# Window attention with an MLP: VectorE does the mean's subtraction ahead of the second low part of U, and the bias addition ahead of the next strip's second maximum

## What is computed

```python
qkv = (xw @ qkv_w + qkv_b)...            # q, k, v of each window
attn = softmax(einsum('bhnd,bhmd->bhnm', q, k) * dh ** -0.5 + bias)
out = einsum('bhnm,bhmd->bhnd', attn, v)... @ proj_w + proj_b
x = x + xr                               # xr: out, put back in image order
xn = layernorm(x, norm2_g, norm2_b)
x = x + gelu(xn @ fc1_w + fc1_b) @ fc2_w + fc2_b
```

## Time and profile before

| | before |
|---|---|
| median of three runs | 1924.84 us (1924.18 to 1928.86) |
| the profiled execution | 1922.45 us |
| its span in the profile | 1920.8 us |
| TensorE busy | 1741.0 us, 91% of the span |
| VectorE busy | 1593.1 us, 83% |
| ScalarE busy | 1536.0 us, 80% |
| GpSimd busy | 1245.8 us, 65% |

### The profile page before, as it was taken

How to read it: one execution, slowest core, us unless ns; L and a number is a source line. 1 busy time by engine, 2 the same in 40 slices (tenths; PEclk the granted TensorE clock), 3 DMA queues, 4 the chain that set the end, 5 groups by cost and what they waited for, 6 DMA issues and landing times. The chain is left out here.

```text
span 1920.8 us, 90622 instructions
## 1 busy us (share of the span) xinstructions
PE 1741.0 (91%) x38180; PEld 1035.6 (54%) x38180; DVE 1593.1 (83%) x2134; ACT 1536.0 (80%) x3090; POOL 1245.8 (65%) x1048
## 2 busy tenths in 40 slices
PE   5999999999999999999999999996999968998996
PEld 3656656665565666656566566651577743333332
DVE  6899889999999999899989999864777757888883
ACT  3788888888888888888888888884666649888881
POOL 5788888888888888888888888763355540221222
PEclk9999999999999999999999999995899985999998
DMA  4343554434444443444444343423488759999994
GB/s 115 90 114 97 151 132 111 111 98 111 102 117 105 106 115 96 117 100 118 102 111 112 101 115 99 98 57 70 112 215 216 214 145 177 240 253 257 263 256 143
DMA packets 233230, 262.25 MB, mean 137 GB/s; under 512 B 167078, under 2 KB 179910, under 8 KB 232710
## 3 DMA queue, kind: packets, MB, share of 16 engines
q1 hardware_dynamic: 217478, 217.47, 46.8%
q0 software_dynamic: 15360, 39.08, 6.7%
HBM read 160.79 MB, written 80.88 MB: 126 GB/s over the span
## 5 line engine op out<-in xcount | busy, mean ns | idle before, releaser
L425 POOL TENSOR_TENSOR shift<-const_b,qmax 113x588 bf16<-113x588 bf16 x256 | 413.9, 1617 | 219.6 <-DVE qmax L520 219.6
L512 DVE TENSOR_TENSOR Ul<-Uf 113x784 bf16<-113x784 f32 x192 | 260.2, 1381 | 0.0
L520 DVE TENSOR_REDUCE qmax<-ps_s 113x12 f32<-113x588 f32 x256 | 195.4, 763 | 50.6 <-PE ps_s L917 46.8
L1537 POOL DMA_DIRECT2D out_rolled<-r_OUT x128 | 63.8, 503 | 264.3 <-DVE r_OUT L1606 264.3
L1378 PE MATMUL conv_ps<-xin,band_now 64*64 64x448 bf16 x2688 | 202.8, 364 | 2.2 <-DVE x_low L1256 2.2
L731 ACT ACTIVATE P<-ps_t 113x588 f32<-113x588 f32 x256 | 170.0, 664 | 39.0 <-PE ps_t L969 36.6
L724 ACT COPY Uf<-ps_m 113x392 f32<-113x392 f32 x384 | 172.8, 485 | 29.7 <-PE ps_m L882 21.6
L741 ACT COPY V<-ps_t 49x192 f32<-49x192 f32 x512 | 168.8, 330 | 8.8 <-PE ps_t L969 2.4
L984 PEld LDWEIGHTS ps_o<-P,V 113*32 113x32 f32 x6144 | 108.0, 109 | 103.4 <-ACT P L731 52.4
L762 ACT ACTIVATE G<-ps_m 128x392 f32<-128x392 f32 x256 | 113.9, 502 | 46.5 <-PE ps_m L1023 46.2
L984 PE MATMUL ps_o<-P,V 113*32 113x49 f32 x6144 | 141.6, 210 | 8.7 <-DVE O L531 2.7
(11 more groups left out here) (233 smaller groups left out, 5324.2 us busy)
## 6 DMA issues: line engine op xcount, KB each, us to landing
xin<-rows_scratch SPq DMA_DIRECT2D x96, 236.0 KB, 3.7
XT<-x_tokens SPq DMA_DIRECT2D x64, 294.0 KB, 3.5
X<-x_windows SPq DMA_DIRECT2D x128, 147.0 KB, 3.3
RS<-rs_scratch SPq DMA_DIRECT2D x128, 147.0 KB, 3.1
XR<-x_windows SPq DMA_DIRECT2D x128, 147.0 KB, 3.1
x_scratch<-x SPq DMA_DIRECT2D x128, 147.0 KB, 3.4
y_scratch<-y POOLq DMA_DIRECT2D x96, 196.0 KB, 2.8
r_RS<-rs_scratch SPq DMA_DIRECT2D x128, 147.0 KB, 4.3
```

Source lines behind the costliest of these rows:

```text
L425: nc.gpsimd.tensor_tensor(shift[:, j % 2], e, m, ALU.mult).then_inc(S["md"], 1)
L512: nc.vector.tensor_tensor(Ul[:, r, h, :], Uf[:, r, h, :], U[0][:, r, h, :], ALU.subtract).then_inc(S["u_lo"], 1)
L520: nc.vector.tensor_reduce(qmax[:, j % 2, :].rearrange("p (b n) -> p b n", b=2), ps_s[0:R, :, 0:2 * HQ].rearrange("p b (n t) -> p b n t", t ...
```

## The change

In VectorE's step, `subtract_mean(prv)` and `u_low(nxt, 1)` change places, and `add_bias(prv)` goes ahead of `query_max(nxt, 1)`, directly behind `u_low(nxt, 2)`. No instruction is added, removed or altered, and no other engine's program is touched.

```diff
                 divide(s, 0)
                 u_low(nxt, 0)
+                subtract_mean(prv)
                 u_low(nxt, 1)
-                subtract_mean(prv)
                 query_max(nxt, 0)
                 divide(s, 1)
                 square(prv)
                 u_low(nxt, 2)
+                add_bias(prv)
                 query_max(nxt, 1)
-                add_bias(prv)
```

## The result

| | before | after |
|---|---|---|
| median | 1924.51 us (4 runs, 1919.32 to 1928.86) | 1955.4 us (4 runs, 1953.0 to 1958.35) |
| the profiled execution | 1922.45 us | 1953.0 us |
| its span | 1920.8 us | 1951.3 us |
| first to last second_residual | 1237.5 us | 1264.5 us |

The ratio is 1.0169 [1.0141, 1.0198]: slower, and by more than the rival on the other side had given (1942). 27.0 of the 30.5 us between the two spans lie in the attention phase. The other 3.5 are in phases whose instructions are the same; between the runs of before the time moves by 9.5.

What follows compares the result with a forecast made beforehand. TensorE was taken to stand twice in fc1 because of VectorE, whose second low part waits for GpSimd's memory use. Profiled 1922.45 - 35.6 - 1 = 1885.9, median 2.4 above: 1888 us; range 1880 to 1932.

Steps and rivals of the forecast that it cites:

- the rival on the other side: Centring on GpSimd takes the memory before the second low part; qmax 0.32 later per strip, 1942 us; chance 0.22.
- Step 1: Attention phase, subtract_mean ahead of the second low part: VectorE gets the memory, qmax starts earlier, 35.6 us gained.
- Step 2: Attention phase, add_bias ahead of the second maximum: fits a VectorE wait, costs 0, gains 0.02 per strip, 1 us.
- the side effect: Early add_bias makes GpSimd's chain 0.2 later, t_mean passes the shift, next divide earlier: 0 to 0.2 gained per strip.
- The mild form of the rival: GpSimd takes the memory first, but add_bias's effect brings low1 forward some 0.2: loss 0.1 per strip, 1930 us.
- The rival "no change": What is won ahead of fc1 is given back before the next strip: 1925 us; chance 0.10.
- 54 strips by 0.66: Size of the subtract_mean move's gain: 54 normal strips, each 0.66 us shorter, 35.6 us in all.

Runs made afterwards that it cites:

- mean_gap: Kernel before with subtract_mean ahead of the second low part, and GpSimd's centring moved behind the third shift, where GpSimd stood idle: 1905.89 us, ratio 0.9901.
- gap_only: Kernel before with only GpSimd's centring moved behind the third shift, VectorE's order unchanged: 1942.22 us, ratio 1.0088.
- mean_only: Kernel before with only subtract_mean moved ahead of the second low part, add_bias in its old place: 1941.97 us, ratio 1.0075.
- bias_only: Kernel before with only add_bias moved ahead of the second maximum: 1936.66 us, ratio 1.0065.
- pause11: Kernel before with subtract_mean ahead of the second low part and eleven tiny GpSimd memsets between low1 and centring: 1921.69 us.
- pause16: Kernel before with subtract_mean ahead of the second low part and sixteen tiny GpSimd memsets between low1 and centring: 1916.81 us, ratio 0.9986.
- halves: Kernel before with only the first half of subtract_mean moved ahead of the second low part: 1911.01 us, ratio 0.993.
- wrap_behind: Kernel before with subtract_mean ahead of the second low part, and GpSimd's two wrap_columns copies moved between low1 and centring: 1963.91 us, ratio 1.0228.
- divide_22: Kernel before with VectorE's order subtract_mean, second divide, second low part, and 22 tiny GpSimd memsets between low1 and centring: 1928.66 us.

## Why the prediction was wrong

**Step 1, the contest for the memory, failed.** The sum put VectorE first with 0.68, on the reading that "what counts seems to be whether VectorE's preceding instruction has started, as if the claim were made then". That rested on one case behind a t_var and one against a divide that had not started, neither with a subtract_mean ahead. The 62 contests of the shift with square, behind a divide, bear the reading out but have no subtract_mean ahead either. And the earlier trace rows lies at the edge: at 38 us a centring was issued 0.16 behind t_var's start and 0.60 ahead of normalise0 in both mean_gap and gap_only; it waited in the one (2.73) and ran in the other (1.31). Here that instruction had started 0.31 ahead of centring (0.47 ahead of the low part), the time of issue was as forecast (0.16 against 0.17), and GpSimd won in every normal strip. Behind subtract_mean the claim comes after the low part's own start, which is the point at which the prediction said its rival decides. Why it comes earlier behind a divide stays open. The rival's price was right: 0.32 a strip, 1942; mean_only measured 1941.97.

The rule of the Trainium skill (SBUF — State Buffer, Who interferes with whom), that the one that issues first gets the shared port pair, gave the right winner here, and by it the sum was 1942. The runs agree with it in all 298 cases behind subtract_mean with GpSimd first. They disagree in both directions. GpSimd also won when it was issued up to 0.12 us after the low part. Behind a divide it lost though it was issued up to 0.15 (centring) and 0.26 (low1) ahead, and behind a t_var though 0.60 ahead.

**Step 2, the side effect, had the wrong sign.** The prediction saw that add_bias, granted at once, makes GpSimd's chain 0.2 later, and that was right (the shift comes 2.95 after the strip's start; 2.73 in the earlier trace rows). It then said that t_mean "would be ahead of the shift" and cheaper. t_mean is issued at 718.32, 0.03 ahead of the shift's 718.35, and yet takes 1.22: it ends behind the shift. So 0.03 ahead isn't enough for VectorE. That fits the offset of the contests behind subtract_mean, but is not shown to be the same thing: when t_mean was issued, GpSimd was still at the small copy of 718.17 (0.22), right behind which the shift came. What depends on t_mean moves by 0.22: normalise0, the maximum of the fourth quarter, GpSimd's x1_low and low1, and centring and the second low part behind low1. bias_only shows that alone, +0.22 a strip. The term was a gain of 0.02 and measured a loss of 0.22. The mild form of the rival (low1 earlier, 0.1 a strip) had the same sign error.

**The range** ended at 1932, with 0.21 for slower; even its left-out 1942 would have missed the two losses together.

**What held, and how far.** Once the low part has the memory, it takes 0.96 and qmax follows, as mean_gap shows. The three full strips at the end of the phase, in which there is no centring any more, show the same in the changed kernel itself. VectorE:

```profile
1261.62 1.04 DVE L587 TENSOR_TENSOR x<-ps_m,x 112x392 f32<-112x392 f32 x2 [1.79 <-PE ps_m L1042]
...
1273.93 0.96 DVE L512 TENSOR_TENSOR Ul<-Uf 113x784 bf16<-113x784 f32 x1
...
1280.71 1.04 DVE L587 TENSOR_TENSOR x<-ps_m,x 112x392 f32<-112x392 f32 x2 [1.79 <-PE ps_m L1042]
```

They are 19.09 apart, close to the 19.05 of the forecast, but that is no measure of the gain, since these strips have no token statistics either. The same three strips of the kernel before are 19.54, 19.52 and 19.06 apart; VectorE's rows of the first:

```profile
1216.09 1.04 DVE L587 TENSOR_TENSOR x<-ps_m,x 112x392 f32<-112x392 f32 x2 [0.19 <-issue]
...
1225.72 3.15 DVE L512 TENSOR_TENSOR Ul<-Uf 113x784 bf16<-113x784 f32 x2
...
1235.63 1.04 DVE L587 TENSOR_TENSOR x<-ps_m,x 112x392 f32<-112x392 f32 x2 [0.20 <-issue]
```

So the reordering wins 0.45 and 0.43 in two of them and nothing in the third, where the low parts weren't held up before either. In the changed kernel's normal strips subtract_mean comes 11.52 after the start with an idle of 0.52 released by TensorE (11.3 and 0.5 were forecast), fc1's first part no longer waits for xc, and add_bias takes 0.61 at once. The rival "no change" is out: from qmax to the next second_residual are 5.89 us (729.78 to 735.67), as before, so that what is lost ahead of fc1 is not given back. Neither is a gain: in a normal strip of mean_gap it is 5.90. The prediction's last part named the outcome: "centring lasts 1.31, the second low part about 2"; its strips of 19.8 to 20.05 lacked only the second loss.

**The size was too kind too:** 54 strips by 0.66. Where the low part does take 0.96, normal strips are 19.2 apart (mean_gap 19.22, pause11 and pause16 19.21), 0.50 to 0.52 less than before. The 0.66 rested on one strip, the one at 1058.67, with its late start of 0.28 counted as gain in full, and no run reached it. The long strips, for which the sum had no term, then took a third to a half of what was left: mean_gap came out 19 us ahead of before and halves 14, not 37.

## What to carry to other kernels

Where two engines issue for the same memory within a few tenths of a microsecond, don't reason out a winner from one or two cases elsewhere in the trace: count all contests that the trace holds, by the instruction that stands ahead, and if there is none with the same one ahead, give neither side more than half. A reordering that brings the two closer together is better made with the competitor moved to a stretch in which the other engine waits anyway (mean_gap), after a look at who waits for what is moved (gap_only, wrap_behind). And when an operation is granted earlier, follow the engine that it displaces for a whole period (here a strip), since its delay can come back at the same contest one step further on.

## What the runs showed of the hardware

- A VectorE instruction issued before a GpSimd one can still get the memory after it: by 0.12 us in pause16 (low part 2.26 instead of 0.96). t_mean, of 14 elements a partition, was issued 0.03 ahead of the shift and took 1.22; t_mean's shortest run in any trace here is 0.17.
- Behind a divide VectorE's claim precedes its own instruction: centring issued 0.12 ahead of the low part waited for it (2.27 instead of 1.31, divide_22), and so did low1 issued 0.26 ahead (2.57 instead of 1.49, mean_only).
- VectorE keeps the memory through instructions that follow each other closely: the shift issued at 730.61 waited for square, the third low part and add_bias, 3.52 us instead of 1.17.
- A low part that was issued 0.26 ahead of centring, while low1 still ran, got the memory next (halves, low part 1.13, centring 2.04), though centring followed low1 without a gap.
- TensorE stops for 0.25 us and more in the middle of its matmuls, 17 times in mean_gap (11.9 us), 14 in halves (10.2), 6 in the kernel before (4.3) and 3 in the kernel after (1.7), and goes on 1.2 to 1.6 us after a 16 KB packet of the instruction queue has landed. That it waits for its program is the likely reading; no run tested it.
